# Attention scores of one-head jobs: the high-by-high product of even and odd key tiles moved to separate halves of TensorE's rows

## What is computed

```python
def attention(q, k, v):          # per batch and head, in chunks of 512 keys
    scores = jnp.einsum('bhqd,bhkd->bhqk', q, k) * 64 ** -0.5
    scores = jnp.where(causal, -jnp.inf, scores)
    p = softmax(scores)
    return jnp.einsum('bhqk,bhkd->bhqd', p, v)

x = x + attention(layernorm(x), ctx, ctx)
weight = einsum('oin,n->oi', sigmoid(pweight) - sigmoid(nweight), exps * sigmoid(mask_weight)) * scale
x = x + einsum('bsi,oi->bso', layernorm(x), weight) + bias
```

## Time and profile before

| | us |
|---|---|
| median of 3 runs | 1179.91 |
| lowest and highest | 1177.99 and 1181.48 |
| the profiled execution, its own time | 1179.6 |
| span of its instructions | 1177.8 |
| outside the span | 1.8 |
| PE busy | 1099.1 |
| PEld busy | 809.3 |
| DVE busy | 996.0 |
| ACT busy | 855.9 |
| POOL busy | 493.5 |

### The profile page before, as it was taken

The page is one execution under the profiler, slowest core; times in us unless marked ns, Lnnn a source line. Parts: engine busy times, 40 slices in busy tenths (PEclk is TensorE's granted clock), DMA queues, the critical chain, the costliest instruction groups (busy, mean ns, idle before and its releaser), DMA issues.

```text
span 1177.8 us, 32049 instructions
## 1 busy us (share of the span) xinstructions
PE 1099.1 (93%) x13092; PEld 809.3 (69%) x13092; DVE 996.0 (85%) x1558; ACT 855.9 (73%) x1764; POOL 493.5 (42%) x510
## 2 busy tenths in 40 slices
PE   4788988999999999999999999999999998999988
PEld 3677755676676777777776777777776676777753
DVE  5766788999988888999989888999989888998961
ACT  6789766778786677777876777878776777777740
POOL 3444424344236654343335655333335664331150
PEclk8899999999999999999999999999999999999989
DMA  9999726675669876656778886676678976664442
GB/s 320 321 322 351 242 73 138 148 160 113 140 121 202 200 169 143 141 140 135 134 132 201 195 162 134 133 153 140 116 149 202 189 169 121 133 119 86 89 84 72
DMA packets 382594, 191.13 MB, mean 162 GB/s; under 512 B 358128, under 2 KB 358128, under 8 KB 378352
## 3 DMA queue, kind: packets, MB, share of 16 engines
q1 hardware_dynamic: 381440, 189.05, 69.9%
q10 hardware_dynamic: 1008, 0.04, 0.1%
HBM read 67.15 MB, written 16.78 MB: 71 GB/s over the span
## 4 chain that ended last, share of the span: by engine, by line
PE 49%; DVE 19%; ACT 13%; DMA 8%; issue 6%; POOL 3%; SPq 2%; ACTq 0%; POOLq 0%; DVEq 0%
PE ffnb L473 16%; PE ptb L434 8%; PE slot L420 5%; PE slot L421 5%; DMA pd<-pd 5%; DVE pd L661 4%; DVE mx L647 4%; ACT p L542 4%; PE obank L454 4%; ACT pd L551 3%; ACT pt L558 3%; PE ffnb L497 3%; PE obank L457 3%; PE obank L455 3%; DVE stats L679 3%
## 5 line engine op out<-in xcount | busy, mean ns | idle before, releaser
L542 ACT ACTIVATE p<-slot,mx 128x512 f32<-128x512 f32 (+7 forms) x512 | 377.0, 744 | 137.2 <-issue 74.3
L647 DVE TENSOR_REDUCE mx<-slot 128x1 f32<-128x640 f32 (+7 forms) x352 | 356.1, 1014 | 31.7 <-PE slot L424 30.8
L473 PE MATMUL ffnb<-wt,yt 128*128 128x512 f16 x1464 | 372.4, 381 | 1.1 <-DMA yt<-y 0.8
L653 DVE SCALAR_TENSOR_TENSOR pt<-ptb,pt 128x512 f16<-128x512 f32 (+1 forms) x504 | 281.6, 598 | 51.4 <-ACT pt L558 49.9
L558 ACT ACTIVATE pt<-ptb 128x512 f16<-128x512 f32 (+1 forms) x504 | 239.8, 526 | 106.1 <-PE ptb L434 105.3
L420 PE MATMUL slot<-kt,qt 128*128 128x128 f16 (+3 forms) x1056 | 267.6, 283 | 7.1 <-DMA qs<-qt 2.5
L421 PE MATMUL slot<-kt,qs 128*128 128x128 f16 (+3 forms) x1056 | 267.6, 283 | 0.0
L883 POOL TENSOR_TENSOR ring<-ring,att 128x256 f32<-128x256 f32 x128 | 93.1, 727 | 393.1 <-DVE att L672 392.9
L434 PE MATMUL ptb<-id,p 128*128 128x128 f32 x1700 | 238.1, 278 | 10.8 <-DVE pt L653 10.6
L473 PEld LDWEIGHTS ffnb<-wt,yt 128*128 128x128 f16 x1464 | 137.3, 98 | 100.3 <-issue 2.5
L454 PE MATMUL obank<-v,pt 128*128 128x64 f16 x1700 | 176.4, 193 | 19.8 <-DVE att L672 12.2
(11 more groups left out here) (94 smaller groups left out, 1529.4 us busy)
## 6 DMA issues: line engine op xcount, KB each, us to landing
ring<-in_x_dram SPq DMA_DIRECT2D x32, 512.0 KB, 4.4
cin<-in_ctx_dram SPq DMA_DIRECT2D x32, 512.0 KB, 4.8
out_dram<-ring SPq DMA_DIRECT2D x32, 512.0 KB, 3.4
qs<-qt SPq DMA_DIRECT2D x124, 128.0 KB, 2.9
v<-in_weights_dram SPq DMA_DIRECT2D x11, 1024.0 KB, 8.7
kt<-in_weights_dram SPq DMA_DIRECT2D x11, 1024.0 KB, 8.0
pd<-in_weights_dram SPq DMA_DIRECT2D x5, 1024.0 KB, 8.0
yt<-in_weights_dram SPq DMA_DIRECT2D x5, 1024.0 KB, 8.6
```

Of the source, the lines that this page charges most:

```text
L473: last = pe.matmul(dst, yt[:, k % 2, a * KT_N + kk, :], wt[:, c, kk, half * 512:half * 512 + 512], start=r == 0, stop=r == 3 * KT_N - 1)
L542: last = nc.scalar.activation(p32[:, j.par, hh * j.keys:(hh + 1) * j.keys], slot[:, j.par, base:base + j.keys], ACT.Exp, bias=mx[:, j.par, ...
L647: nc.vector.tensor_reduce(mx[:, j.par, 0:j.heads], src[:, 0:j.heads, 0:j.keys], AX_X, ALU.max, negate=True).then_inc(mx_ready, 1)
L653: nc.vector.scalar_tensor_tensor(pt[:, j.par, j.blocks + blocks.start:j.blocks + blocks.stop, :], ptb[:, c % 2, 0:P * len(blocks)].rearran ...
```

## The change

In words:

- Key tiles with an odd number hold their high part in rows 64 to 127 and the low part in rows 0 to 63; even ones stay as they were. This is done by the engines that write `v16`, which now choose the columns by `high_cols(t)` and `low_cols(t)`.
- In a one-head job, high by high is computed alone, on 64 rows: for even key tiles from `qt` on rows 0 to 63, for odd ones from `qs` on rows 64 to 127. These matmuls are issued alternately, even and odd, ahead of the rest of the job. The two mixed products follow as one matmul on 128 rows for each run (`qs` for even tiles, `qt` for odd ones). Low by low is dropped in these jobs.
- In a job of two or four heads all four partial products stay, but even and odd key tiles are now separate runs.
- In `slot` the even key tiles of a job come first and the odd ones after them (`key_order`). In a one-head job `base` shifts them so that the even ones end at the border of the first bank and the odd ones begin in the second. The maximum, the exponentials and `values` follow that order.
- Only the first matmul into a bank has `start` set.

```diff
+def high_cols(t):
+    return slice(D * (t % 2), D * (t % 2) + D)
+        self.base = 512 - P * (self.i // 2 + 1) if self.heads == 1 else 0
...
+                def high_by_high(odd):
+                    rows = slice(D * odd, D * odd + D)
+                    queries = (qs if odd else qt[:, t % 2])[rows, j.head0, :]
+                    out = []
+                    for n, p0, p1 in runs(odd):
+                        at, dst = columns(0, odd, n, slice(p0, p1))
+                        out.append((at // 512, dst, queries, kt16[rows, p0:p1:2, j.head0, :]))
+                    return out
...
+                if j.heads == 1:
+                    one, other = high_by_high(0), high_by_high(1)
+                    for k in range(max(len(one), len(other))):
+                        issue(one[k:k + 1])
+                        issue(other[k:k + 1])
                 for hh in range(j.heads):
-                    h, base = j.head0 + hh, hh * HEAD_STRIDE[i]
-                    first = 0
-                    while first <= i:
-                        place = (place0 + first) % K_PLACES
-                        end = min(i + 1, first // 4 * 4 + 4, first + K_PLACES - place)
-                        dst = slot[:, j.par, base + first * P:base + end * P]
-                        keys = kt16[:, place:place + end - first, h, :]
-                        pe.matmul(dst, qt[:, t % 2, h, :], keys, start=True, stop=False, skip_group_check=True)
-                        last = pe.matmul(dst, qs[:, h, :], keys, start=False, stop=end <= i,
-                                         skip_group_check=True)
-                        first = end
+                    h = j.head0 + hh
+                    for odd in range(2):
+                        for n, p0, p1 in runs(odd):
+                            at, dst = columns(hh, odd, n, slice(p0, p1))
+                            keys = kt16[:, p0:p1:2, h, :]
+                            if j.heads > 1:
+                                issue([(at // 512, dst, (qs if odd else qt[:, t % 2])[:, h, :], keys)])
+                            pe.matmul(dst, (qt[:, t % 2] if odd else qs)[:, h, :], keys, start=False, stop=True,
+                                      skip_group_check=True)
...
-                    for blk in range(j.i + 1):
+                    for blk, c in enumerate(key_order(j.i)):
                         k = hh * (j.i + 1) + blk
-                        v = v16[:, (j.t - j.i + blk) % V_PLACES, h]
+                        v = v16[:, (j.t - j.i + c) % V_PLACES, h]
...
-                nc.scalar.copy(v16[:, t % V_PLACES, :, 0:D], cin[:, :].rearrange("p (h d) -> p h d", d=D)
+                nc.scalar.copy(v16[:, t % V_PLACES, :, high_cols(t)], cin[:, :].rearrange("p (h d) -> p h d", d=D)
```

More of the change, by code:

```diff
@@ L41, with key_order, low_cols @@
 PAIRS = 6
+def key_order(i):
+    return list(range(0, i + 1, 2)) + list(range(1, i + 1, 2))
+def high_cols(t):
+    return slice(D * (t % 2), D * (t % 2) + D)
+def low_cols(t):
+    return high_cols(t + 1)
 class Job:
@@ L411, in scores @@
                 place0 = t - i
-                for hh in range(j.heads):
-                    h, base = j.head0 + hh, hh * HEAD_STRIDE[i]
-                    first = 0
-                    while first <= i:
-                        place = (place0 + first) % K_PLACES
-                        end = min(i + 1, first // 4 * 4 + 4, first + K_PLACES - place)
-                        dst = slot[:, j.par, base + first * P:base + end * P]
-                        keys = kt16[:, place:place + end - first, h, :]
-                        pe.matmul(dst, qt[:, t % 2, h, :], keys, start=True, stop=False, skip_group_check=True)
-                        last = pe.matmul(dst, qs[:, h, :], keys, start=False, stop=end <= i,
-                                         skip_group_check=True)
-                        first = end
-                    last = pe.matmul(slot[:, j.par, base + i * P:base + (i + 1) * P], idb[:, :], maskb[:, :],
-                                     start=False, stop=True, skip_group_check=True)
+                started = set()
@@ new lines, in runs, with columns @@
+                def runs(first):
+                    out = []
+                    for n, c in enumerate(range(first, i + 1, 2)):
+                        place = (place0 + c) % K_PLACES
+                        if out and out[-1][2] == place - 1:
+                            out[-1][2] = place + 1
+                        else:
+                            out.append([n, place, place + 1])
+                    return out
+                def columns(hh, odd, n, places):
+                    at = j.base + hh * HEAD_STRIDE[i] + P * (n + odd * (i // 2 + 1))
+                    return at, slot[:, j.par, at:at + P * ((places.stop - places.start + 1) // 2)]
@@ new lines, in high_by_high, with issue @@
+                def high_by_high(odd):
+                    rows = slice(D * odd, D * odd + D)
+                    queries = (qs if odd else qt[:, t % 2])[rows, j.head0, :]
+                    out = []
+                    for n, p0, p1 in runs(odd):
+                        at, dst = columns(0, odd, n, slice(p0, p1))
+                        out.append((at // 512, dst, queries, kt16[rows, p0:p1:2, j.head0, :]))
+                    return out
+                def issue(products):
+                    for bank, dst, queries, keys in products:
+                        pe.matmul(dst, queries, keys, start=bank not in started, stop=False, skip_group_check=True)
+                        started.add(bank)
@@ new lines, in scores @@
+                if j.heads == 1:
[3 more added lines that the diff above has]
+                        issue(other[k:k + 1])
+                for hh in range(j.heads):
+                    h = j.head0 + hh
[7 more added lines that the diff above has]
+                                      skip_group_check=True)
+                    at, dst = columns(hh, i % 2, i // 2, slice(0, 1))
+                    last = pe.matmul(dst, idb[:, :], maskb[:, :], start=False, stop=True, skip_group_check=True)
@@ L449, in values @@
                     h = j.head0 + hh
-                    for blk in range(j.i + 1):
+                    for blk, c in enumerate(key_order(j.i)):
                         k = hh * (j.i + 1) + blk
-                        v = v16[:, (j.t - j.i + blk) % V_PLACES, h]
+                        v = v16[:, (j.t - j.i + c) % V_PLACES, h]
                         dst = oacc[:, h % GROUP, :]
-                        pe.matmul(dst, turned[:, k, :], v[:, 0:D], start=blk == 0, stop=False, skip_group_check=True)
-                        pe.matmul(dst, turned[:, k, :], v[:, D:2 * D], start=False, stop=False,
+                        pe.matmul(dst, turned[:, k, :], v[:, high_cols(c)], start=blk == 0, stop=False,
                                   skip_group_check=True)
-                        last = pe.matmul(dst, turned[:, j.blocks + k, :], v[:, 0:D], start=False, stop=blk == j.i,
-                                         skip_group_check=True)
+                        pe.matmul(dst, turned[:, k, :], v[:, low_cols(c)], start=False, stop=False,
+                                  skip_group_check=True)
+                        last = pe.matmul(dst, turned[:, j.blocks + k, :], v[:, high_cols(c)], start=False,
+                                         stop=blk == j.i, skip_group_check=True)
                 last.then_inc(pv_done, 1)
@@ L540, in exponentials @@
                 for hh in range(j.heads):
-                    base = hh * HEAD_STRIDE[j.i]
+                    base = j.base + hh * HEAD_STRIDE[j.i]
                     last = nc.scalar.activation(
@@ L646, in maxima @@
                 src = slot[:, j.par, :].rearrange("p (h c) -> p h c", c=HEAD_STRIDE[j.i])
-                nc.vector.tensor_reduce(mx[:, j.par, 0:j.heads], src[:, 0:j.heads, 0:j.keys], AX_X, ALU.max,
+                nc.vector.tensor_reduce(mx[:, j.par, 0:j.heads], src[:, 0:j.heads, j.base:j.base + j.keys], AX_X, ALU.max,
                                         negate=True).then_inc(mx_ready, 1)
@@ L863, in c_split @@
                 v = v16[:, t % V_PLACES]
-                nc.gpsimd.tensor_tensor(v[:, :, D:2 * D], cin[:, :].rearrange("p (h d) -> p h d", d=D),
-                                        v[:, :, 0:D], ALU.subtract).then_inc(c_lo, 1)
+                nc.gpsimd.tensor_tensor(v[:, :, low_cols(t)], cin[:, :].rearrange("p (h d) -> p h d", d=D),
+                                        v[:, :, high_cols(t)], ALU.subtract).then_inc(c_lo, 1)
             def y_split(k):
```

7 lines of the change are left out of this document (4 added, 3 removed).

## The result

The changed kernel takes 1185.46 us, median of 14 runs (1182.63 to 1186.28), the kernel before 1180.62 us in as many (1176.5 to 1182.81). The ratio is 1.0039 with a 95% interval of 1.0027 to 1.0052: slower by 0.4%, where 1160.5 us and a gain were forecast. The profiled execution has a span of 1184.1 us against 1177.8. All medians in this document are of executions at a granted clock of 0.94 or more; one of e3's twelve had 0.66, took 1588.7 us and is left out.

The account below looks back on a forecast made before the run. PE was taken as the bound, DVE close behind. 38.4 us less stream minus 14.8 us for mode changes gave 23.6 us, of which DVE let 19.1 through: 1179.6 - 19.1 = 1160.5 us, range 1148 to 1226.

Parts of the forecast that it names:

- The change of mode: Two switches between 128-row and 64-row matmuls per one-head job, 512 in all, taken at 29 ns each: 14.8 us more.
- the rival of a drain in part: Each mode change in one-head jobs costs 50 to 100 ns, gain and cost nearly cancel: 1171 to 1193 us; chance 0.15.
- The break-even of 75 ns: Cost per mode change at which 512 changes use up the 38.4 us cut from PE's stream.
- The saved columns: Score columns removed in one-head jobs, i = 4 to 7, by streaming both row halves at once: 39.2 us less.
- the wraps of t = 29 and 31: Where the key ring wraps, unlike even and odd runs make one half wait: one tile less saved, 2 us taken off.
- The rival in which they don't: The second 64-row matmul waits for the first, so no columns are saved: 1181 us, or 1196 with 29 ns changes; chance 0.09.
- That PE's stream sets the pace: PE leads in every stage, DVE next; of 23.6 us less stream, 19 us was to show in the time.
- the full-drain rival: The array runs empty at each mode change in one-head jobs, up to 164 ns, passed in full: 1225 us; chance 0.26.
- The free-mode rival: Mode changes cost nothing, PE 38.4 us shorter, DVE becomes the bound with i = 7: 1152 us; chance 0.20.
- What was set at nothing: Column choice in `v16`, the key-transposing DMA, order in `values`, DVE's maximum and ACT's exponentials: zero change each.
- The split runs, counted at 0.9 us: In stages with i = 1 to 3, one or two more matmul pairs a head at 2.3 ns a matmul: 0.9 us more.
- The signs named beforehand: PE timeline, windows and waits: starts within 0.03 us, i = 7 stage 45.3 us, longer PE waits; gap over 0.075 us refutes.

Follow-up runs that it names:

- e3: The changed kernel with the 64-row products only in the stages with i = 7, four products on 128 rows in the others: 1183.31 us.
- e5: The changed kernel with all four partial products on 128 rows in every job, new layout and split runs kept: 1185.29 us.
- e8: The changed kernel with one-head high by high computed on 128 rows for even key tiles only, left out for odd ones: 1175.55 us.
- e6: The kernel before with only the swapped high and low halves of odd key tiles, scores as before: 1179.21 us.
- e7: The kernel before with only the split even and odd runs, their order and shifted base, four products on 128 rows: 1183.35 us.
- e2: The kernel before with one extra matmul of 64 columns on 64 rows at the head of each one-head job's scores: 1203.95 us.
- e12: The changed kernel with the 64-row matmuls moved to the end of a job's scores, ahead of the product with the values: 1185.56 us.
- e13: e2 with two trips per one-head job instead of one (64 columns on 64 rows, on 128, on 64 again): 1267.24 us.

## Why the prediction was wrong

**The change of mode.** The bound, zero to 164 ns, held; the value taken, 29 ns, did not: 96 ns in, 93 to 103 ns out and 10 ns in the matmul behind. It was chosen because every change of kind in the trace was free, but none of those changes alters which rows work together, so they were no neighbours of this one. The term measured 54 us instead of 14.8: this is the first step that failed, and it turned a stream that was to be 23.6 us shorter into one that is 13 us longer. The Trainium skill's sentence, a change of tiling mode drains TensorE ("TensorEngine Tiling (Array Packing)", Key Properties), agrees with the held-back weight loads, the size being 60% of the upper bound. The break-even of 75 ns, worked out in the rival, was right for PE's stream. Nearest to what happened is the rival of a drain in part, 50 to 100 ns, with 1171 to 1193 us, which had been given 0.15: a change costs 105 ns, just above its price, and the time lies inside its range, but only because most of the cost was hidden, which it had not foreseen.

**The saved columns.** 41 us where 39.2 were worked out: the 2 us taken off for the wraps of t = 29 and 31, where in-order issue was to leave one half waiting for the other, were not lost, since each half went on by itself. The halves overlap to 3 to 4 ns. The rival in which they don't is dead.

**That PE's stream sets the pace.** This is the other step that failed, and it stood ahead of all sums. Had only the 29 ns been put right, the sum would have been 1179.6 - 38.4 + 54 = 1195 us; had only the share been put right, a quarter of 23.6 us, 1174; the full-drain rival, which let everything pass, had 1225. Measured are 1185.5, by the experiments 5 us for the layout (e5), 10 off for the columns (e8) and 10 on for the mode changes. In the stages with i of 4 and more PE leads by a hair, with DVE and the round through ACT right behind: a quarter of the saving passes (e8: 10 of 41 us against e5), as does about a fifth of the cost (e8 to the changed kernel: 10 of 54 us). The prediction let through 80%, by the argument that DVE was 84 to 93% busy and could go to 95 or 97. Rows 3 and 7 held a hint: DVE at 93% with i = 7 and at 94% with t = 18, and no stage of this kernel has it higher. With t = 18 PE never stops, though, so that row can't tell whether DVE could do more; e8 does, with 94% beside an idle PE. The free-mode rival, 1152 us, fails for the same reason; e8 has 1175.6.

**What was set at nothing.** For the work of DVE and ACT it held: 998.3 and 857.8 us busy against 996.0 and 855.9. The swapped halves did cost nothing (e6). The split runs, counted at 0.9 us, cost 3 to 5 us (e5, e7), as much as the whole result; this step was mis-sized, and its cause is open.

**The signs named beforehand.** Starts within 0.03 us of each other came. A gap over 0.075 us at either end of the 64-row group, named as what would prove the prediction wrong, came at both ends. The stage with i = 7 was to last 45.3 us and lasts 46.9. PE's waits for DVE were to grow and shrank instead, as its stream grew; in e8, where it shrank, they grew. DVE's maximum is as long as before (1.21 us for 1024 columns).

## What to carry to other kernels

Half-row matmuls in two row halves do run at once, but here each group of them costs 0.21 us at its two ends, as much as 500 columns. The columns saved in one group have to be well over that; here they were 512 at best and 256 at least. Before an engine's work is cut, ask how much slack its followers have, and don't count it up to 100%: here the follower stayed at 94% of a stage, its busiest share in the trace of before, even with the leader idle (e8). And the cheapest test of whether an engine sets the pace is to give it a little more to do: 14 us of dummy matmuls cost nothing here.

## What was not expected of the hardware

A change between matmuls on 128 and on 64 rows holds back the weight load and the matmul behind it by 96 ns on the way in (behind 512 fp16 and 128 bf16 columns; e2, e12) and 93 to 103 ns on the way out, and each time anew (e13). The first 128-row matmul after it takes 10 ns more; where that is the one matmul between two groups, the way in is 107 ns (e13). A 16-bit weight load that was not issued ahead delays its matmul by only 4 ns. Two matmuls on different halves of the rows, each with its own weight load, start 3 to 4 ns apart and stream at full rate into different PSUM banks. Each half of the rows keeps its own order only: with t = 28 to 31 a matmul of the odd half starts ahead of one of the even half that was issued before it.
